# Conv stack on one core: the next image's tiles stream through a ring of eight buffers, and the last update is written in place

## What is computed

```
x = x + L0(gn(x))     # 1x1 mixing, leaky relu, min-max over the image
x = x + L1(gn(x))     # complex 3x3 convolution in the Fourier domain
x = x + L2(gn(x))     # 8-bit quantised 3x3 convolution, zero padded
x = x + L3(gn(x))     # 3x3 circular convolution (written with FFTs in the reference)
```

```
x_q = round(clip(gn(x) / scale_input, -127, 127))      # scale_input from the maximum over all images
out = conv3x3(x_q, weight_int8) * (scale_input * scale_weight) + bias
```

## Time and profile before

| | us |
|---|---|
| median of 3 runs | 6232.46 (6221.11 to 6239.16) |
| the profiled execution's own time | 6232.09 |
| its span, first to last instruction | 6230.2 |
| `rstd` of image 0, start of the seven joint stages | 4228.4 |
| `rstd` of image 7, their end | 6045.2 |
| one joint stage, mean of 7 | 259.5 |

### The profile page before, as it was taken

One profiled execution on the slowest core, in us unless ns is written; L12 is line 12 of the kernel. 1 busy time (PEld: TensorE's weight loads), 2 busy tenths in 40 slices (PEclk: granted clock), 3 DMA queues, 4 the chain that ended last, 5 costly groups with the idle time before them and its releaser, 6 DMA issues. The chain is left out here.

```text
span 6230.2 us, 202732 instructions
## 1 busy us (share of the span) xinstructions
PE 5335.2 (86%) x63882; PEld 3402.6 (55%) x63882; DVE 5053.6 (81%) x10660; ACT 4538.9 (73%) x8793; POOL 3153.6 (51%) x5676
## 2 busy tenths in 40 slices
PE   0379979979979979979989989968898988989889
PEld 0058748748748748747757757833343433434334
DVE  5879979979979989988998998986676766767664
ACT  2578768868868867867876666768787877878775
POOL 3178768758858858858857858921111110111102
PEclk9889989989989989999999999989999999999999
DMA  6516616616616625625624524646676766767665
GB/s 203 158 47 209 204 40 206 207 46 201 206 53 190 208 69 171 208 88 159 206 95 115 159 84 113 177 94 155 166 204 163 204 162 159 200 162 196 168 163 139
DMA packets 535621, 958.88 MB, mean 154 GB/s; under 512 B 121946, under 2 KB 126938, under 8 KB 532826
## 3 DMA queue, kind: packets, MB, share of 16 engines
q1 hardware_dynamic: 467546, 798.95, 45.0%
q10 hardware_dynamic: 67456, 151.01, 7.8%
HBM read 560.40 MB, written 287.60 MB: 136 GB/s over the span
## 5 line engine op out<-in xcount | busy, mean ns | idle before, releaser
L1655 PE MATMUL pC<-xs,taps 128*128 128x512 f16 x4608 | 1095.8, 383 | 106.7 <-DMA xhalo<-xs 100.4
L981 PE MATMUL pM<-gw,xh 64*128 64x256 f16 (+1 forms) x24960 | 1130.7, 244 | 5.5 <-DVE yt L1141 4.7
L981 PEld LDWEIGHTS pM<-gw,xh 64*128 64x128 f16 x24960 | 972.5, 95 | 133.4 <-issue 12.0
L1551 POOL TENSOR_TENSOR xn<-xn,one_col 128x1 f32<-128x1 f32 x520 | 170.4, 328 | 1406.4 <-ACT xn L1585 1406.4
L1655 PEld LDWEIGHTS pC<-xs,taps 128*128 128x128 f16 x4608 | 449.3, 98 | 672.1 <-DVE xs L1705 90.2
L1571 ACT ACTIVATE scaled<-X,qbias,qscale 128x512 f32 (+1 forms) x512 | 413.3, 808 | 327.8 <-DMA X<-after_layer 297.0
L742 POOL TENSOR_TENSOR X<-X,zo 128x256 f32 (+1 forms) x512 | 372.5, 727 | 548.3 <-DVE zo L1105 548.3
L279 PE MATMUL pM<-X,mix0s 64*64 64x512 f32 x2304 | 530.1, 634 | 134.5 <-DVE X L1073 108.5
L723 POOL TENSOR_TENSOR X<-X,rl 128x512 f32 x384 | 478.4, 1275 | 270.8 <-ACT rl L772 270.7
L1593 ACT ACTIVATE xs<-xn 128x1028 f16<-128x1028 f32 x520 | 546.8, 1051 | 86.7 <-POOL xn L1552 86.2
L1712 DVE SCALAR_TENSOR_TENSOR result<-pC,X 128x512 f32<-128x512 f32 x512 | 352.4, 688 | 303.3 <-DMA out_dram<-result 181.4
(11 more groups left out here) (249 smaller groups left out, 13574.2 us busy)
## 6 DMA issues: line engine op xcount, KB each, us to landing
gw<-row_weights SPq DMA_DIRECT2D x520, 288.0 KB, 3.4
after_layer<-X SPq DMA_DIRECT2D x512, 256.0 KB
out_dram<-result SPq DMA_DIRECT2D x512, 256.0 KB
X<-in_x_dram SPq DMA_DIRECT2D x448, 256.0 KB
X<-after_layer ACTq DMA_DIRECT2D x224, 512.0 KB, 5.7
stage<-in_x_dram SPq DMA_DIRECT2D x192, 512.0 KB
xhalo<-xs SPq DMA_DIRECT2D x504, 96.4 KB, 3.7
qhalo<-q SPq DMA_DIRECT2D x496, 96.2 KB, 3.9
```

The costliest lines, as they stand in the source:

```text
L981: nc.tensor.matmul(pY[:, r, col:col + nd * P], row(xh, r)[:, k, p, ri, off:off + P], weights(r, q_, d, nd, ri), start=ri == 0 and off == 1 ...
L1655: nc.tensor.matmul(bank, taps3[:, d, wh], xs[:, h, own, d:d + W], start=d == 0 and n == 0, stop=False)
```

## The change

1. `DELAY` goes from 12 to 6, so a stage has 77 turns. Layer-2 slots keep their old numbering through `second(k, g)`.
2. Tiles of the next image no longer go straight into `X`. A new buffer `stream` has `RING` = 8 slots. `scale2` reads `stream` (for image 0, `X`), and `update` reads `stream` and writes its sum to `X`.
3. `load` moves from ACT to SP. It is one tile per DMA and stands last in SP's turn, behind the halos and the store. It is issued in turn t for tile w = t - DELAY + 2, which `scale2` takes in turn t + 2, and waits for `x3_ready` of tile w - 8, the last reader of that slot.
4. `finish` writes into `X` in place of `result`, and no longer waits for a store. The store reads `X`. `update` of tile w waits instead for the store of tile w of the image before.
5. `scaled` has two buffers in place of four; the unused output of `square3` goes to a PSUM bank in fp32 in place of bf16 in SBUF; the zeros for the image's border come from DRAM, so one memset goes.

```
-        DELAY = 12
+        DELAY = 6
+        AHEAD = 12
-                scaled = sb("scaled", [P, 4, W], f32, pm)
+                scaled = sb("scaled", [P, 2, W], f32, pm)
+                stream = sb("stream", [P, RING, W], f32, pm)
-                result = sb("result", [P, 4, W], f32, pm)
+                unused = ps("unused2", [P, W], pm)
+                def second(k, g):
+                    n = k + AHEAD - DELAY
+                    return n % RING, g + n // RING
 # SP
+                    def store(b, v, k, g):
                         tile, slot = v - 1, (k - 9) % 4
+                        wait_alone(sp, out_stored[slot], (b * (J // 4) + n + 1) * 16, passed)
                         sp.wait_ge(x4_ready, b * J + v)
-                        sp.dma_start(out[b]...[tile], result[:, slot]).then_inc(out_stored[slot], 16)
+                        sp.dma_start(out[b]...[tile], Xf[:, tile]).then_inc(out_stored[slot], 16)
+                    def load(b, w, k):
+                        slot = (k - 2) % RING
+                        wait_alone(sp, x3_ready, b * J + w - 7, passed)
+                        sp.dma_start(stream[:, slot], x2s[b]...[:, w]).then_inc(loaded2[slot], 16)
                     def both(b, c3, c2):
                         def step(t, k, g):
                             ...
                             if c3 and live(t, 9, J + 9):
-                                store(b, t - 8, k)
+                                store(b, t - 8, k, g)
+                            if c3 and c2 and live(t, DELAY - 2, DELAY - 2 + J):
+                                load(b + 1, t - DELAY + 2, k2)
 # ACT
-                        nc.scalar.activation(scaled[:, k % 4], Xf[:, w], ACT.Identity, ...)
+                        nc.scalar.activation(scaled[:, k % 2], Xf[:, w] if first else stream[:, slot], ACT.Identity, ...)
-                    def load(b, w, k, g):
-                        slot = (k - 10) % 4 // 2
-                        wait_alone(act, x4_ready, (b - 1) * J + w + 2, passed)
-                        wait_alone(act, loaded2[slot], (b * (J // 4) + 2 * g - 3 + (k + 2) // 4) * 16, passed)
-                        act.dma_start(Xf[:, bass.ds(w, 2)], x2s[b]...[:, bass.ds(w, 2)]).then_inc(loaded2[slot], 16)
 # DVE
+                        if not first:
+                            dve.wait_ge(out_stored[(k - 2) % 4], ((b - 1) * (J // 4) + n + 2) * 16)
-                        ...(out=Xf[:, w], in0=pC2[:, (k - 2) % 4], scalar=oscale2[:, :], in1=Xf[:, w], ...
+                        ...(out=Xf[:, w], in0=pC2[:, (k - 2) % 4], scalar=oscale2[:, :],
+                            in1=Xf[:, w] if first else stream[:, (k - 2) % RING], ...
-                        dve.wait_ge(out_stored[slot], (b * (J // 4) + n + 1) * 16)
-                        ...(out=result[:, slot], in0=pC3[:, (k - 1) % 2], scalar=OUT_SCALE3, in1=Xf[:, tile], ...
+                        ...(out=Xf[:, tile], in0=pC3[:, (k - 1) % 2], scalar=OUT_SCALE3, in1=Xf[:, tile], ...
```

More of the change, by code:

```diff
@@ L1441, in program @@
                 out_stored = [s_(f"out_stored{k}") for k in range(4)]
-                loaded2 = [s_(f"loaded2_{k}") for k in range(2)]
+                loaded2 = [s_(f"loaded2_{k}") for k in range(RING)]
                 CONV2_CREDIT = RING - 1
@@ L1564, in _, with scale2 @@
                 def _(act):
[L1565 to L1571, removed]
+                    def scale2(b, w, k, g, first):
+                        slot = (k + 4) % RING
+                        if not first:
+                            n = w // RING if isinstance(w, int) else g - 2 + (k + 4) // RING
+                            wait_alone(act, loaded2[slot], ((b - 1) * (J // RING) + n + 1) * 16, passed)
+                        if not (isinstance(w, int) and w < 2):
+                            wait_alone(act, q_ready, b * J + w - 1, passed)
+                        nc.scalar.activation(scaled[:, k % 2], Xf[:, w] if first else stream[:, slot], ACT.Identity, bias=qbias[:, bass.ds(b, 1)],
                                              scale=qscale[:, bass.ds(b, 1)]).then_inc(scaled_ready, 1)
                     def square3(b, j, k):
-                        act.wait_ge(sq3_done, b * J + j + 1)
+                        act.wait_ge(sq3_done, b * J + j + 2)
                         act.wait_ge(x3_ready, b * J + j + 1)
-                        nc.scalar.activation(unused[:, k % 2], Xf[:, j], ACT.Square, bias=bias2[:, :],
+                        nc.scalar.activation(unused[:, :], Xf[:, j], ACT.Square, bias=bias2[:, :],
                                              accum_out=sq3[:, bass.ds(j, 1)]).then_inc(sq3_done, 1)
@@ L1605, in step @@
                             u = t - DELAY
+                            k2, g2 = second(k, g)
                             if c2 and live(u, 0, J):
-                                scale2(b + 1, u, k, g)
+                                scale2(b + 1, u, k2, g2, not c3)
                             if c3 and live(t, 1, ITEMS + 1):
@@ L1667, in step @@
                             if c2 and live(w, 0, J):
-                                conv2(b + 1, w, k, g)
+                                conv2(b + 1, w, *second(k, g))
                             if c3 and live(v, 1, J + 1):
@@ L1693, in quant, with update @@
                         dve.wait_ge(conv2_done, b * J + w + 1)
-                        nc.vector.tensor_scalar(q[:, (k + 5) % RING, 1:W + 1], scaled[:, k % 4], MAGIC, -MAGIC, ALU.add,
+                        nc.vector.tensor_scalar(q[:, (k + 5) % RING, 1:W + 1], scaled[:, k % 2], MAGIC, -MAGIC, ALU.add,
                                                 ALU.add).then_inc(q_ready, 1)
-                    def update(b, w, k):
+                    def update(b, w, k, g, first):
                         dve.wait_ge(conv2_done, b * J + w + 1 + CONV2_CREDIT)
-                        nc.vector.scalar_tensor_tensor(out=Xf[:, w], in0=pC2[:, (k - 2) % 4], scalar=oscale2[:, :], in1=Xf[:, w],
+                        if not first:
+                            n = w // 4 if isinstance(w, int) else 2 * g - 5 + (k + 2) // 4
+                            dve.wait_ge(out_stored[(k - 2) % 4], ((b - 1) * (J // 4) + n + 2) * 16)
+                        nc.vector.scalar_tensor_tensor(out=Xf[:, w], in0=pC2[:, (k - 2) % 4], scalar=oscale2[:, :],
+                                                       in1=Xf[:, w] if first else stream[:, (k - 2) % RING],
                                                        op0=ALU.mult, op1=ALU.add,
@@ L1717, in step @@
                             u, v = t - DELAY, t - 7
+                            k2, g2 = second(k, g)
                             if c3 and live(v, 1, J + 1):
[L1719 removed]
+                                finish(b, v, k)
                             if c2 and live(u, 6, J + 6):
[L1721 removed]
+                                update(b + 1, u - 6, k2, g2, not c3)
                             if c2 and live(u, 0, J):
[L1723 removed]
+                                clip(b + 1, u, k2)
                             if c3 and live(t, 1, ITEMS + 1):
```

41 lines of the change are left out of this document (17 added, 24 removed).

## The result

The changed kernel took 6873.83 us (6864.81 to 6877.41), the kernel before 6232.55 us. The ratio is 1.103 (95% interval 1.1011 to 1.1048), so it is 10% slower. The forecast was 6730 us, in a range of 6480 to 6980.

The account below looks back on a forecast made before the run. Joint stages were taken as PE-bound, DMA loops next. The moved load's loop of 9.8 us per two turns, less 6 us saved edge time, lengthens seven stages from 259.5 to 331 us: 500 us on 6232.1, 6730 us, range 6480 to 6980.

Parts of the forecast that it names:

- two-turn loop: In joint stages, DVE, SP, DMA, ACT and DVE again take 9.8 us per two turns, 4.9 per turn against PE's 3.47.
- The landing: SP's 256 KB load: 4.2 us, near 96 KB transfers (3.8 to 4.0), under 512 KB at a stage's head (4.53).
- L: Time from the load's issue on SP's queue to ACT's start: taken as 4.2 us, ends 2.7 and 5.7.
- With 4.9 us turns it goes away: DVE's wait for stores, 168.5 us before and inherited by `update`, vanishes in the slower turns and frees nothing.
- The gain of the shorter delay: Six turns fewer per joint stage save edge time in which PE waits: 6 us per stage, 42 us in all.
- As late as the ring allows: Reading of SP's load against the DMA rule to issue early: four issues on one sequencer, load latest possible; no separate size.
- The smaller edits: PSUM output of the square, two `scaled` buffers, one memset less: taken as 0; `scaled` might cost up to 13 us.
- PE's clock: In the slower joint turns, PE busy 3.47 of 4.9 us, the granted clock was expected to stay at 2.4 GHz.
- The short landing: Rival: SP's load lands in 2.7 us, loops of 8.3 us, 6400 us; chance 0.09 with all up to the forecast.
- The long one: Rival: the load queues behind store and halos on SP's queue, takes 5.7 us, 7063 us in all; chance 0.06.
- the load could be hidden: Rival: PE sets the joint stages' pace and the overlap's gain stays, 6190 or 6078 us; chance 0.09.
- No net change: Rival: SP's issues overlap more and saved turns pay for late loads, about 6230 us; chance 0.04.

Follow-up runs that it names:

- e1: Changed kernel with the load first in SyncE's turn, ahead of halos and store: 6213.3 us, 0.9968 of the kernel before.
- e2: Changed kernel with load and store swapped in SyncE's turn, halos still first: 6321.3 us, 1.0142 of the kernel before.
- e4: Changed kernel with each load bringing only the first 256 of 512 columns, 128 KB: 6739.6 us, 1.0813 of the kernel before.
- e7: Changed kernel with the load, same tile and wait, issued by ACT at the end of its turn: 6114.5 us, 0.9817 of the kernel before.
- e8: Kernel before with only its two-tile load moved from ACT to SyncE, behind the even turn's store: 7238.7 us, 1.1622 of the kernel before.
- e9: The kernel of e7 (load issued by ACT) with DELAY 12 in place of 6: 6189.2 us, 0.9937 of the kernel before.
- e10: The kernel of e7 again, in more rounds and on the same chip as e9: 6111.7 us, 0.9809 of the kernel before.
- e3: Changed kernel with DELAY back at 12, all else kept: 7025.2 us, 1.1277 of the kernel before.

## Why the prediction was right, and where its sizes were off

**The mechanism** was that of the forecast: the two-turn loop of `low`, SP's turn, landing, `scale2`, `high`, `low`. e1, e2, e4, e7 and e8 each change one link of it, and the pace follows. Term by term for even turns, forecast and measured median: `low` to issue 3.1 and 3.3; issue until ACT starts 4.2 and 4.7 (4.4 to landing, 0.3 until ACT starts); `scale2` to the end of `low` 2.5 and 2.49; two turns 9.8 and 10.5 (5.23 per turn). "The even turns set the pace" was not borne out: odd turns lack `quant` (3.0 to the issue), but their loads take 4.8 until ACT starts, 10.4 in all.

**The landing** is the term that was mis-sized. The prediction took it between a smaller transfer and a calmer hour, "near the 96 KB row and under the 4.53", and gave the 256 KB store 1.1 us ahead of it no price of its own. e2 shows that price: 1.5 us of the 4.4. The 0.7 us per loop, 0.5 of it the landing and 0.2 SP's part, make 18 us per stage over the 27 loops from turn 10 to 64; turns 4 to 10 were 4 us shorter than the sum had them (turn 10 at 31.2 in place of 35.4), since the first loads, with no store ahead, land in 2.6 to 2.7 us. The ends of the forecast don't quite fit its own 22 us per 0.1 us of L: 6525 and 6965 belong to L of 3.3 and 5.3, not 5.2.

**The last turns.** "With 4.9 us turns it goes away", the prediction says of the store's wait. It does in the steady turns, but not at the end of a stage, where turns are short again. DVE after, the last turns of the stage before `rstd` at 4590.9, beside the earlier trace rows:

```profile
4583.71 0.75 DVE L1707 SCALAR_TENSOR_TENSOR X<-pC,oscale,stream 128x512 f32<-128x512 f32 x1 [1.69 <-DMA out_dram<-X]
...
4585.42 0.75 DVE L1707 SCALAR_TENSOR_TENSOR X<-pC,oscale,stream 128x512 f32<-128x512 f32 x1 [0.95 <-DMA out_dram<-X]
...
4587.15 0.75 DVE L1707 SCALAR_TENSOR_TENSOR X<-pC,oscale,stream 128x512 f32<-128x512 f32 x1 [0.97 <-DMA out_dram<-X]
```

Updates are 1.7 us apart in place of 0.87, about 4 us per stage. In all a stage is 350.2 and not 331: 18 less 4 by turn 64, 4 behind it, and the 1 us by which 332 had been rounded down. That is 19.2 us, times seven 134; the 9.7 us by which the stages began later make up the rest of the 144 us by which the forecast was short.

**The gain of the shorter delay** was put at 6 us per stage and is 11 to 12 (e9 against e10). The prediction had taken about a quarter of the idle edge time; it was half. In the changed kernel the shorter delay is worth more, 22 us per stage (e3), and is hidden in a stage that is still 91 us longer than before.

**"As late as the ring allows"** was a misreading. The slot of tile w is freed by `update` of tile w - 8, which in the changed kernel belongs to the very turn of the load (w + 4), so the ring of eight allows no earlier turn. Late is only the load's place within SP's turn, and with the same ring and the same wait e7 is faster than the kernel before.

**The smaller edits** cost nothing that shows. The square takes 0.67 us into PSUM in place of 0.71 into SBUF. The Trainium skill says that an ACTIVATE is faster to PSUM than to SBUF ("ScalarE: Activation LUTs", section "Step-by-step: what each stage is for"), and this trace agrees, though the output's type changed with its place (fp32 in place of bf16), so the 0.04 us can't be put down to the place alone. ACT was not the bound, so it gained nothing.

**PE's clock** was expected at 2.4 GHz in the slower turns too. The stretch view after, in the middle of a stage (window, length, busy us of the engines, PE clock, DMA share, GB/s), beside the earlier trace rows:

```profile
4720.00:4760.00 40.00, 30.96 (x123) 12.04 (x122) 21.69 (x48) 25.28 (x40) 3.76 (x16) 0.91 0.59 137
```

0.91 is a mean of two levels. At 4734.44 and 4755.13 PE's nine `conv3` products took 3.80 and 3.74 us at 1.2 GHz, where at 2.4 GHz they take 2.1; ahead of each PE had stood idle for 2.3 and 2.4 us. In the joint stages after, the granted clock was 1.2 GHz for 474 of 2452 us, before for 185 of 1817. The prediction was wrong here, but it cost next to no time in the steady turns: two turns with such a spell in them took 10.46 us on average, those without 10.42, since there PE is not what the loop waits for.

**The rivals.** The short landing (2.7 until ACT starts) is near what e2 has by another order, 3.1. The long one (5.7) is near what e8 has with 512 KB. That the load could be hidden was given 0.09: not in this order of SP's turn, but in e7, and nearly in e1, with the same wait and the same lead of two turns. No net change would have needed 1.5 us until ACT starts; no kernel here has a median landing under 2.9.

## What to carry to other kernels

When a DMA moves to another engine's list, ask which wait stands ahead of it there, how many turns lie between that wait and the use, and add up the whole loop: wait, issues ahead, landing, consumer, back to the wait; divided by the turns it spans, it is the pace if it exceeds the bound. A transfer on which the pipeline depends goes ahead of stores, since a store costs it both the issue, if they share a list (1.2 us here), and the data in front of it (1.5 us); e10 suggests that another engine's list saves it the first and not the second. And when one list is always late, first place in a turn is last place in the turn before: count turns, not positions.

## What the runs showed of the hardware that was not expected

- A 256 KB load issued 1.2 us behind a 256 KB store on the same queue landed in 4.4 us; the same load ahead of the store, in 2.9 us. With 128 KB behind the store it took 3.8 us. On ScalarE's queue, less than 2 us behind a store on SP's, a 256 KB load took 4.9 us on the median (e10).
- ACT issued a DMA before two activations that stand ahead of it in its program had run (issue at 5102.14, the activations at 5102.54 and 5103.25). SP shows the opposite case: its list holds nothing but issues and waits, and a DMA there is never earlier than the waits ahead of it.
- The granted PE clock fell to 1.2 GHz for short spells, those shown above behind idle stretches of 2.3 and 2.4 us. The stretch from which the prediction concluded otherwise was itself not steady: from 4140 to 4220 us the granted clock was 1.00 before and 0.95 after, though PE was a little busier there (53.4 of 80 us in place of 51.4).
